# Attention and FP4 feed-forward kernel: the mask of the transposed scores moved from TensorE to VectorE

## The chip, the cores and the metric

The kernel runs on one core of one Trainium2 chip. The metric is the device time of one execution in microseconds (us). A core has five engines with queues of their own: TensorE (PE; its weight loads are listed as PEld), VectorE (DVE), ScalarE (ACT), GpSimd (POOL) and SyncE (SP), which here only issues DMAs. They wait for each other by semaphores alone.

## The reference

`x` has 8 batches of 1024 rows of 512. With `xn` the layer norm of `x`, the result is `x + attention(xn) + ffn(xn)`.

```
qkv = xn @ W_attn + b_attn                    # 16 heads of 32
att = einsum('bhqd,bhkd->bhqk', q, k) * 32 ** -0.5
att = softmax(where(causal, att, -inf))
y   = einsum('bhqk,bhkd->bhqd', att, v)       # then @ W_proj + b_proj
ffn = fp4(silu(fp4(xn, w_gate)) * fp4(xn, w_up), w_down)
```

`fp4` quantises both of its operands in blocks of 16. The feed-forward part comes after the attention in the kernel and the change does not touch it.

## The kernel before, in words

`attention` loops over 8 batches. A batch first projects q, k and v, and then works through 8 pairs of heads (`PAIRS`), one after the other; after the last pair come the output projection and the start of the next batch. The order of the work in each engine is written out by hand in the engine's block.

For each pair the softmax needs two forms of the scores. The first gives the row maxima: for each of 16 tiles (`TILE`: 2 heads, 8 blocks of 128 queries, in the order of blocks 4, 3, 5, 2, 6, 1, 7, 0) `scores` (L727) computes 128 queries against all keys up to the diagonal, adds the causal mask by a matmul of an identity in bfloat16 with `causal`, which holds -1e30 above the diagonal (L747), and VectorE reduces the tile to minus its maximum (`row_max`, L494, reduction at L498). Two places in PSUM alternate: even tiles use `ps_s` (up to 1024 columns), odd ones `ps_dense[:, 0]` (up to 512). When a pair's 16 maxima are there, TensorE transposes them (`maxima`, L750), VectorE splits them into a high and a low part (`split_max`, L501), and two DMAs on SyncE's queue put them as two more rows under q (L321).

The second form is transposed, keys by queries, and has the maxima in it, so that ScalarE can take the exponential at once. For each of 8 steps (`kt`, a block of 128 keys; in the engines' loops the unit `u`) `transposed_scores` (L754) makes the parts listed in `PARTS`: per head up to 512 queries each, 4 parts in steps 0 to 3 and 2 parts in steps 4 to 7, 24 in all. The part that holds the diagonal block gets the mask by a further bfloat16 matmul (L764). The parts go through a ring of 3 PSUM banks (`ps_st`), from which ScalarE writes the exponentials (L663): for steps 0 to 4 into a ring of 3 places in SBUF (`pt`), for steps 5 to 7 into places of their own (`rob`). The parts with the higher queries come first, the diagonal block comes last.

The exponentials have two readers: `times_v` (L767, matmul at L776) multiplies them by v, step by step, steps 5 to 7 during the next pair; and the denominators are their sums over the keys. GpSimd adds the exponentials of steps 0 to 4 up in `stage` (`sum_up`, L422, additions at L434, a copy of the first block at L431), then `denominators` (L780, matmul at L793) sums that and steps 5 to 7 over the partitions in unit 1 of the next pair. VectorE copies the result out of PSUM (`copy_den`, L509, L515), DMAs spread it, VectorE inverts it (`invert`, L519), DMAs spread the inverse, and `divide` (L526, L535) scales the product in unit 7.

In the loop over units each engine takes its share of several pairs: while pair p's transposed scores are made, `beside(p, u)` deals the maxima's tiles of the pairs ahead, two per unit (`SHARE`): the last 8 tiles of pair p + 1 in units 0 to 3, the first 8 of pair p + 2 in units 4 to 7 (`M_UNIT` is 3). In pair 7 VectorE also normalises four tiles of the next batch's x (`norm`, L473, L475), in pair 6 it takes their statistics (`stats`, L464).

## Time and profile before

| | us |
|---|---|
| median of 3 runs (4161.25 to 4167.64) | 4165.79 |
| the profiled execution | 4181.09 |
| its span, first to last instruction | 4179.3 |
| TensorE busy | 3883.4 |
| VectorE busy | 2601.6 |
| ScalarE busy | 1221.1 |
| GpSimd busy | 930.7 |

The span is the time between the first and the last instruction of the program; the execution's own time adds what lies around it. Busy times are sums over the whole span, attention and feed-forward together; matmuls overlap each other in the records, so that TensorE's busy time is no measure of how full it is. The granted clock of TensorE is given as a share of full speed: 1.00 is 2.4 GHz, 0.5 is 1.2 GHz. In a row of the timeline, "x3" stands for three like instructions that were merged, and the square brackets tell how long the engine sat idle before and which instruction released it.

### The profile page before, as it was taken

The page shows a single profiled execution, that of the slowest core. Times are in us where ns is not written, and L with a number is a line of the kernel's source. Part 1 is how long each engine was busy: PE and PEld are TensorE (multiplying, and loading weights), DVE is VectorE, ACT ScalarE, POOL GpSimd, SP SyncE. Part 2 cuts the span into 40 slices and gives each one's busy share as a digit, 9 for nine tenths or more (in the row PEclk, how much of TensorE's full clock was granted, in tenths as well). Part 3 has the DMA queues.
Part 4 walks back from the last instruction along what each step waited for, and adds up shares of the span by engine and source line. Part 5 has one row for each costly group of instructions (what it writes and reads, how often), then busy time and mean ns, then how long its engine had stood idle before and what let it go on. Part 6 is the DMA issues. An engine that isn't in the chain of part 4 may idle for free. (4 is left out here: it accounts for less than half of the span.)

```text
span 4179.3 us, 63450 instructions
## 1 busy us (share of the span) xinstructions
PE 3883.4 (93%) x21836; PEld 2759.2 (66%) x21836; DVE 2601.6 (62%) x3683; ACT 1221.1 (29%) x2295; POOL 930.7 (22%) x464
## 2 busy tenths in 40 slices
PE   7999999999999999999999934999999999999998
PEld 5556556556556565565565523888888888888887
DVE  4554654654654645645545477777777777777776
ACT  2341441432432423513414422222222222222221
POOL 0451550551542533613514500000000000000000
PEclk9999999999999999999998956999999999999999
DMA  4414324324325234234144121110011000100010
GB/s 152 105 47 152 91 62 152 87 73 142 74 90 138 71 105 128 56 129 119 41 152 93 44 76 43 31 32 30 30 35 33 30 30 30 37 31 30 30 35 28
DMA packets 161754, 302.38 MB, mean 72 GB/s; under 512 B 41072, under 2 KB 43120, under 8 KB 161520
## 3 DMA queue, kind: packets, MB, share of 16 engines
q1 hardware_dynamic: 143088, 265.79, 22.7%
q10 hardware_dynamic: 18432, 33.56, 2.5%
q8 instruction: 135, 2.21, 0.2%
q14 instruction: 99, 0.81, 0.1%
HBM read 196.61 MB, written 101.13 MB: 71 GB/s over the span
## 5 line engine op out<-in xcount | busy, mean ns | idle before, releaser
L1252 PE MATMUL f_ps<-wgu,xqt 128*128 128x512 f32 (+1 forms) x4608 | 992.5, 373 | 17.4 <-DVE h L1107 14.6
L1252 PEld LDWEIGHTS f_ps<-wgu,xqt 128*128 128x128 f32 x4608 | 841.1, 188 | 153.8 <-DVE h L1107 30.0
L498 DVE TENSOR_REDUCE mx<-ps_s 128x1 f32<-128x640 f32 (+3 forms) x576 | 552.5, 959 | 288.0 <-PE ps_s L747 281.1
L663 ACT ACTIVATE pt<-ps_st 128x512 f32<-128x512 f32 (+3 forms) x1152 | 549.3, 527 | 613.8 <-PE ps_st L764 381.2
L434 POOL TENSOR_TENSOR stage<-stage,pt 128x1536 f32<-128x1536 f32 (+2 forms) x176 | 518.0, 2943 | 16.5 <-ACT pt L663 1.1
L1262 PE MATMUL f_ps_o<-wd,hqt 128*128 128x512 f32 x2112 | 512.4, 395 | 2.2 <-DVE hqt L1114 2.2
L1262 PEld LDWEIGHTS f_ps_o<-wd,hqt 128*128 128x128 f32 x2112 | 392.6, 189 | 80.9 <-DVE hqt L1114 2.6
L722 PE MATMUL ps_dense<-arena,wa 128*128 128x512 f32 x1536 | 399.9, 406 | 9.5 <-DVE rob L546 8.0
L498 DVE TENSOR_REDUCE mx<-ps_dense 128x1 f32<-128x512 f32 x448 | 218.7, 488 | 247.7 <-PE ps_dense L747 247.7
L722 PEld LDWEIGHTS ps_dense<-arena,wa 128*128 128x128 f32 x1536 | 283.4, 191 | 74.3 <-issue 12.2
L761 PE MATMUL ps_st<-stack 98*128 98x512 f32 (+3 forms) x768 | 315.4, 440 | 5.1 <-ACT pt L663 5.1
L761 PE MATMUL ps_st<-arena 98*128 98x512 f32 (+3 forms) x768 | 299.1, 432 | 17.5 <-ACT pt L663 16.1
L434 POOL TENSOR_TENSOR stage<-pt 128x1792 f32<-128x1792 f32 x64 | 257.2, 4019 | 101.3 <-ACT pt L663 101.3
L638 ACT ACTIVATE stage<-ps_dense,bqk 128x512 fp32r<-128x512 f32 x128 | 88.1, 689 | 604.4 <-PE ps_dense L722 604.4
L431 POOL TENSOR_TENSOR stage<-pt,ones 128x256 f32<-128x256 f32 x64 | 39.3, 614 | 999.5 <-ACT pt L663 603.6
L764 PE MATMUL ps_st<-identb,causal 128*128 128x128 bf16 x1024 | 248.0, 243 | 0.0
L761 PEld LDWEIGHTS ps_st<-arena 98*128 98x128 f32 x768 | 149.1, 207 | 138.2 <-ACT pt L663 89.3
L745 PE MATMUL ps_s<-stack 96*128 96x512 f32 (+1 forms) x576 | 185.3, 396 | 56.9 <-DVE mx L498 30.7
L857 PE MATMUL ps_dense<-wp,yt 128*128 128x512 f32 x512 | 224.5, 594 | 2.1 <-DVE rob L546 2.0
L1182 ACT ACTIVATE silu<-f_ps 128x512 f32<-128x512 f32 (+1 forms) x192 | 107.0, 557 | 373.7 <-PE f_ps L1252 373.7
L761 PEld LDWEIGHTS ps_st<-stack 98*128 98x128 f32 x768 | 152.7, 213 | 95.3 <-ACT pt L663 53.0
L663 ACT ACTIVATE rob<-ps_st 128x384 f32<-128x384 f32 (+2 forms) x384 | 144.8, 384 | 207.1 <-PE ps_st L764 202.8
(121 smaller groups left out, 5044.1 us busy)
## 6 DMA issues: line engine op xcount, KB each, us to landing
qk_scratch<-stage SPq DMA_DIRECT2D x128, 512.0 KB, 3.0
stack<-qk_scratch SPq DMA_DIRECT2D x192, 256.0 KB
arena<-qk_scratch SPq DMA_DIRECT2D x192, 256.0 KB
xs<-in_L_attn_x SPq DMA_DIRECT2D x64, 256.0 KB, 3.1
rob<-in_L_attn_x ACTq DMA_DIRECT2D x64, 256.0 KB, 2.8
acc_scratch<-rob ACTq DMA_DIRECT2D x64, 256.0 KB, 2.2
xt<-in_L_attn_x SPq DMA_DIRECT2D x64, 256.0 KB, 2.6
at<-acc_scratch SPq DMA_DIRECT2D x64, 256.0 KB, 2.6
```

The lines of the kernel that those rows point to most:

```text
L434: nc.gpsimd.tensor_tensor(both[:, :, cols], (ring(0) if kt == 1 else both)[:, :, cols], ring(kt)[:, :, cols], ALU.add).then_inc(summed_up, 1)
L498: nc.vector.tensor_reduce(mx[:, h * ST + q:h * ST + q + 1], scores_bank(p, n)[:, 0:(q + 1) * P], axis=AX.X, op=ALU.max, negate=True).then_ ...
L638: nc.scalar.activation(stage[:, i % 2, 0].bitcast(F32R), bank("QK", i), ACT.Identity, bias=bqk[:, r * G + g:r * G + g + 1]).then_inc(qk_hi, 1)
L663: nc.scalar.activation(a[:, q - first * P:q - first * P + n], ps_st[:, w % ST_RING, 0:n], ACT.Exp, scale=SCALE).then_inc(st_exp, 1)
L722: last = nc.tensor.matmul(bank(*use), left(lh, k), right(rh, k), start=n == 0, stop=n == len(terms) - 1)
L745: last = nc.tensor.matmul(out[:, k0:k1], qs, stack(p)[0:KS, 2 + h, k0:k1], start=True, stop=k1 < keys)
L761: last = nc.tensor.matmul(out, stack(p)[0:KM, 2 + h, kt * P:(kt + 1) * P], stack(p)[0:KM, h, q:q + n], start=True, stop=not diagonal)
L764: last = nc.tensor.matmul(out[:, 0:P], causal[:, :], identb[:, :], start=False, stop=True)
L857: last = nc.tensor.matmul(bank("P", k), yt[:, g, t * P:(t + 1) * P], wp[:, g, :], start=g == 0, stop=g == G - 1)
L1182: nc.scalar.activation(silu[:, c, 0:n], ps[:, [0, 1, 1][c], 0, 0:n], ACT.Silu).then_inc(s_done, 1)
L1252: last = nc.tensor.matmul(ps[:, [0, 1, 1][c], gu, 0:n], xqt[:, a, k], wgu[:, b, gu, k, f:f + n], start=i == 0, stop=i == len(terms) - 1)
L1262: last = nc.tensor.matmul(ps_o[:, :], hqt[:, a, k], wd[:, b, k], start=i == 0, stop=i == len(terms) - 1)
```

## The change

- `transposed_scores` makes one matmul per part; the masks at L764 are gone. In their place VectorE takes, after the exponential, the minimum of the diagonal blocks of both heads (2 x 128 columns) and a constant `seen` in bfloat16, which is 0 where a key lies behind the query and the largest number elsewhere (`clean`). `times_v` and `sum_up` wait for it.
- The parts with the lower queries, and so the diagonal block, come first in `PARTS`.
- The exponentials of steps 0 to 3 have fixed places, step 4 takes step 1's. ScalarE waits for the readers of each place; GpSimd sums in the order 1, 0, 2, 3, 4.
- The maxima's masks are a function of their own (`mask_scores`) and follow the scores later: behind another part, or two tiles' masks one after the other.
- The tiles are dealt as 2, 3, 3, 2, 2, 2, 2, 0 per unit, `M_UNIT` is 2; the split of the maxima and the inversion come in unit 3, the normalisations of pair 7 in unit 2.
- ScalarE instead of VectorE copies the denominators.

```diff
@@ -41,12 +42,17 @@
     PARTS = [[(h, max(c * QC, kt * P), (c + 1) * QC - max(c * QC, kt * P))
-              for c in reversed(range(NQ)) if (c + 1) * QC > kt * P for h in range(2)] for kt in range(ST)]
+              for c in range(NQ) if (c + 1) * QC > kt * P for h in range(2)] for kt in range(ST)]
     NPARTS = sum(len(parts) for parts in PARTS)
     PART0 = [sum(len(parts) for parts in PARTS[:kt]) for kt in range(ST + 1)]
-    ST_RING, PT_RING, SLOTS, XR = 3, 3, 4, 4
+    ST_RING, SLOTS, XR = 3, 4, 4
     RINGED = 5
+    PT0 = {}
+    for kt in range(RINGED - 1):
+        PT0[kt] = 2 * P * sum(ST - k for k in range(kt))
+    PT0[RINGED - 1] = PT0[1]
+    PT_COLS = 2 * P * sum(ST - k for k in range(RINGED - 1))
     TAIL0 = {kt: 2 * P * sum(ST - k for k in range(RINGED, kt)) for kt in range(RINGED, ST)}
...
@@ -54,19 +60,22 @@
+    SUM_ORDER = [1, 0, 2, 3, 4]
+    FREED = {0: 2, 1: 1, 2: 3, 3: 4, 4: 5}
     SUMS = sum(summed(p) for p in range(PAIRS))
     TILE = [(h, q) for h in range(2) for t in range(ST // 2) for q in (ST // 2 + t, ST // 2 - 1 - t)]
-    SHARE = TILES // ST
-    M_UNIT = ST // 2 - 1
-    EARLY = TILES - SHARE * (M_UNIT + 1)
+    SHARE = [2, 3, 3, 2, 2, 2, 2, 0]
+    M_UNIT = 2
+    EARLY = TILES - sum(SHARE[:M_UNIT + 1])
     DEN_UNIT = 1
     def beside(p, u):
-        first = TILES + EARLY + p * TILES + SHARE * u
-        return [divmod(n, TILES) for n in range(first, first + SHARE) if n < PAIRS * TILES]
+        first = TILES + EARLY + p * TILES + sum(SHARE[:u])
+        return [divmod(n, TILES) for n in range(first, first + SHARE[u]) if n < PAIRS * TILES]
...
@@ -399,6 +408,8 @@
             pool.wait_ge(consts, 2)
+            pool.affine_select(out=seen[:, :], in_=seen[:, :], compare_op=ALU.is_ge, fill=0.0,
+                               base=0, pattern=[[1, P]], channel_multiplier=-1).then_inc(consts, 1)
             pool.wait_ge(b_load, 4 * DMA)
...
@@ -422,26 +433,27 @@
                     pool.wait_ge(st_exp, ONE + b * PAIRS * NPARTS + p * NPARTS + PART0[kt + 1])
+                    pool.wait_ge(cleaned, ONE + b * PAIRS * ST + p * ST + kt + 1)
                     if kt > 1:
                         pool.wait_ge(summed_up, ONE + b * SUMS + p * RINGED + kt)
+                    both = stage[:, :, :, :].rearrange("p h a n -> p h (a n)")
                     cols = slice(kt * P, S)
-                    both = stage[:, :, :, :].rearrange("p h a n -> p h (a n)")
-                    ring = lambda k: pt[:, (p * RINGED + k) % PT_RING]
                     if kt == 0:
-                        nc.gpsimd.tensor_tensor(both[:, :, 0:P], ring(0)[:, :, 0:P], ones[:, 0:1].unsqueeze(2).to_broadcast([P, 2, P]),
+                        nc.gpsimd.tensor_tensor(both[:, :, 0:P], exps(0)[:, :, 0:P], ones[:, 0:1].unsqueeze(2).to_broadcast([P, 2, P]),
                                                 ALU.mult).then_inc(summed_up, 1)
+                    elif kt == 1:
+                        nc.gpsimd.tensor_tensor(both[:, :, cols], exps(0)[:, :, cols], exps(1), ALU.add).then_inc(summed_up, 1)
                     else:
-                        nc.gpsimd.tensor_tensor(both[:, :, cols], (ring(0) if kt == 1 else both)[:, :, cols], ring(kt)[:, :, cols],
-                                                ALU.add).then_inc(summed_up, 1)
+                        nc.gpsimd.tensor_tensor(both[:, :, cols], both[:, :, cols], exps(kt), ALU.add).then_inc(summed_up, 1)
                         inv_std(b + 1, 0, XR)
-                    for kt in range(summed(p)):
-                        if kt == 0 and p:
-                            pool.wait_ge(den_full, ONE + b * PAIRS + p)
+                    if p:
+                        pool.wait_ge(den_full, ONE + b * PAIRS + p)
+                    for kt in SUM_ORDER[:summed(p)]:
                         sum_up(p, kt)
...
@@ -506,13 +518,11 @@
-                def copy_den(p):
-                    if p == 0:
-                        dve.wait_ge(o_out[0], ONE + b * (ST // 2) * DMA)
-                    else:
-                        dve.wait_ge(y_div, ONE + b * PAIRS * 2 + p * 2)
-                    dve.wait_ge(den_full, ONE + b * PAIRS + p + 1)
-                    nc.vector.tensor_copy(dn, den_bank(p)).then_inc(den_copy, 1)
+                def clean(p, kt):
+                    dve.wait_ge(st_exp, ONE + b * PAIRS * NPARTS + p * NPARTS + PART0[kt] + 2)
+                    nc.vector.tensor_tensor(exps(kt)[:, :, 0:P], exps(kt)[:, :, 0:P], seen[:, :].unsqueeze(1).to_broadcast([P, 2, P]),
+                                            ALU.min).then_inc(cleaned, 1)
...
@@ -581,17 +591,22 @@
                         tiles = beside(p, u)
+                        if u == M_UNIT + 1 and p + 1 < PAIRS:
+                            split_max(p + 1)
+                        late = len(PARTS[u]) == 2
+                        if late and len(PARTS[u - 1]) == 2:
+                            clean(p, u - 1)
                         for n in tiles[:1]:
                             row_max(*n)
-                        if u == DEN_UNIT and p:
-                            copy_den(p - 1)
+                        if not late:
+                            clean(p, u)
                         for n in tiles[1:]:
                             row_max(*n)
-                        if u == M_UNIT and p + 1 < PAIRS:
-                            split_max(p + 1)
-                        if u == M_UNIT and p:
+                        if u == ST - 1:
+                            clean(p, u)
+                        if u == M_UNIT + 1 and p:
                             invert(p - 1)
-                        if p == PAIRS - 2 and not final and u > M_UNIT:
+                        if p == PAIRS - 2 and not final and 0 <= u - M_UNIT - 1 < XR:
                             stats(b + 1, u - M_UNIT - 1)
...
@@ -645,11 +660,13 @@
                     for kt in range(ST):
-                        before = p * RINGED + kt - PT_RING
-                        if kt < RINGED and before >= 0:
-                            pp, pk = divmod(before, RINGED)
-                            act.wait_ge(pv_done, ONE + b * PAIRS * ST + pp * ST + pk + 1)
-                            act.wait_ge(summed_up, ONE + b * SUMS + pp * RINGED + max(pk, 1) + 1)
+                        if kt == RINGED - 1:
+                            act.wait_ge(pv_done, ONE + b * PAIRS * ST + p * ST + 2)
+                            act.wait_ge(summed_up, ONE + b * SUMS + p * RINGED + FREED[1])
+                        elif kt < RINGED and p:
+                            last = RINGED - 1 if kt == 1 else kt
+                            act.wait_ge(pv_done, ONE + b * PAIRS * ST + (p - 1) * ST + last + 1)
+                            act.wait_ge(summed_up, ONE + b * SUMS + (p - 1) * RINGED + FREED[last])
                         if kt == RINGED:
...
@@ -658,9 +675,15 @@
                             w = p * NPARTS + PART0[kt] + i
-                            a, first = exps(p, kt, h)
+                            if kt == DEN_UNIT and p and i == len(PARTS[kt]) - 1:
+                                if p == 1:
+                                    act.wait_ge(o_out[0], ONE + b * (ST // 2) * DMA)
+                                else:
+                                    act.wait_ge(y_div, ONE + b * PAIRS * 2 + (p - 1) * 2)
+                                act.wait_ge(den_full, ONE + b * PAIRS + p)
+                                nc.scalar.activation(dn, den_bank(p - 1), ACT.Copy).then_inc(den_copy, 1)
                             act.wait_ge(st_full, ONE + b * PAIRS * NPARTS + w + 1)
-                            nc.scalar.activation(a[:, q - first * P:q - first * P + n], ps_st[:, w % ST_RING, 0:n], ACT.Exp,
+                            nc.scalar.activation(exps(kt)[:, h, q - kt * P:q - kt * P + n], ps_st[:, w % ST_RING, 0:n], ACT.Exp,
                                                  scale=SCALE).then_inc(st_exp, 1)
...
@@ -742,10 +767,13 @@
                         k1 = min(k0 + 512, keys)
-                        last = nc.tensor.matmul(out[:, k0:k1], qs, stack(p)[0:KS, 2 + h, k0:k1], start=True,
+                        nc.tensor.matmul(out[:, k0:k1], qs, stack(p)[0:KS, 2 + h, k0:k1], start=True,
                                                 stop=k1 < keys)
-                    last = nc.tensor.matmul(out[:, q * P:keys], identb[:, :], causal[:, :], start=False, stop=True)
-                    last.then_inc(s_full, 1)
+                def mask_scores(p, n):
+                    h, q = TILE[n]
+                    nc.tensor.matmul(scores_bank(p, n)[:, q * P:(q + 1) * P], identb[:, :], causal[:, :], start=False,
+                                     stop=True).then_inc(s_full, 1)
...
@@ -756,31 +784,27 @@
                     pe.wait_ge(st_exp, ONE + b * PAIRS * NPARTS + max(w - ST_RING + 1, 0))
-                    out = ps_st[:, w % ST_RING, 0:n]
-                    diagonal = q == kt * P
-                    last = nc.tensor.matmul(out, stack(p)[0:KM, 2 + h, kt * P:(kt + 1) * P],
-                                            stack(p)[0:KM, h, q:q + n], start=True, stop=not diagonal)
-                    if diagonal:
-                        last = nc.tensor.matmul(out[:, 0:P], causal[:, :], identb[:, :], start=False, stop=True)
-                    last.then_inc(st_full, 1)
+                    nc.tensor.matmul(ps_st[:, w % ST_RING, 0:n], stack(p)[0:KM, 2 + h, kt * P:(kt + 1) * P],
+                                     stack(p)[0:KM, h, q:q + n], start=True, stop=True).then_inc(st_full, 1)
                     pe.wait_ge(st_exp, ONE + b * PAIRS * NPARTS + p * NPARTS + PART0[kt + 1])
+                    pe.wait_ge(cleaned, ONE + b * PAIRS * ST + p * ST + kt + 1)
                     for s in range(2):
                             last = nc.tensor.matmul(by_tile(y_bank(p)[y_rows(h, s), y_cols(kt, s)]), v_head(kt, p, h),
-                                                    exps_of_parity(p, kt, h, s), start=kt == 0, stop=kt == ST - 2 + s)
+                                                    exps_of_parity(kt, h, s), start=kt == 0, stop=kt == ST - 2 + s)
                     last.then_inc(pv_done, 1)
                     if p + 2 < PAIRS:
-                        pe.wait_ge(s_max, ONE + b * PAIRS * TILES + (p + 2) * TILES + EARLY + SHARE * DEN_UNIT)
+                        pe.wait_ge(s_max, ONE + b * PAIRS * TILES + (p + 2) * TILES + EARLY + sum(SHARE[:DEN_UNIT]))
                     for kt in range(summed(p) - 1, ST):
...
@@ -816,22 +840,29 @@
                     scores(1, n)
+                    mask_scores(1, n)
                 for p in range(PAIRS):
                         parts = len(PARTS[u])
-                        early = (parts + 1) // 2
-                        for i in range(early):
+                        ahead = 2 if u == M_UNIT else 1
+                        for i in range(parts // 2):
                             transposed_scores(p, u, i)
+                            if u == M_UNIT and i < ahead:
+                                for n in tiles[i:i + 1]:
+                                    scores(*n)
                         if u == M_UNIT + 1 and p + 1 < PAIRS:
                             maxima(p + 1)
-                        for n in tiles[:1]:
-                            scores(*n)
-                        for i in range(early, parts):
-                            if i < parts - 1 or parts == 2:
-                                transposed_scores(p, u, i)
+                        if u != M_UNIT:
+                            for n in tiles[:ahead]:
+                                scores(*n)
+                        if parts > 2:
+                            transposed_scores(p, u, 2)
+                        for n in tiles[:ahead]:
+                            mask_scores(*n)
                         if u == DEN_UNIT and p:
...
@@ -839,10 +870,11 @@
                             times_v(p, u - 1)
-                        if parts > 2:
-                            transposed_scores(p, u, parts - 1)
-                        for n in tiles[1:]:
+                        transposed_scores(p, u, parts - 1)
+                        for n in tiles[ahead:]:
                             scores(*n)
+                        for n in tiles[ahead:]:
+                            mask_scores(*n)
                 for kt in range(RINGED, ST):
```

## Rows read from the trace of the kernel before

**Rows 1.** The page: span, and busy time of the engines with share and instructions.
```profile
span 4179.3 us, 63450 instructions
...
PE 3883.4 (93%) x21836; PEld 2759.2 (66%) x21836; DVE 2601.6 (62%) x3683; ACT 1221.1 (29%) x2295; POOL 930.7 (22%) x464
```

**Rows 2.** Windows of one pair and of one batch: us, PE, PEld, DVE, ACT, POOL busy, PEclk.
```profile
178.20:202.00 23.80, 22.68 (x173) 13.01 (x169) 14.57 (x23) 10.91 (x24) 13.38 (x6) 0.93 0.36 81
1370.50:1392.70 22.20, 21.09 (x171) 12.21 (x169) 14.54 (x23) 10.91 (x24) 13.34 (x6) 1.00 0.40 88
...
432.60:734.90 302.30, 287.18 (x1753) 174.71 (x1753) 159.75 (x248) 102.18 (x216) 116.07 (x56) 0.93 0.36 99
734.90:1028.30 293.40, 278.66 (x1753) 170.70 (x1754) 159.79 (x248) 102.04 (x216) 116.06 (x56) 0.97 0.37 102
```

**Rows 3.** Groups by line: count | busy us, mean ns | idle before, releaser.
```profile
L764 PE MATMUL ps_st<-identb,causal 128*128 128x128 bf16 x1024 | 248.0, 243 | 0.0
```

**Rows 4.** Timeline of pair 2, TensorE: start us, us, engine, line, operation.
```profile
174.35 0.48 PE L745 MATMUL ps_dense<-arena 96*128 96x512 f32 x1
...
174.72 0.48 PE L761 MATMUL ps_st<-arena 98*128 98x512 f32 x1
...
179.43 0.71 PE L761 MATMUL ps_st<-arena 98*128 98x512 f32 x2
```

**Rows 5.** VectorE groups by shape: two reductions, an operation on SBUF alone.
```profile
L498 DVE TENSOR_REDUCE mx<-ps_s 128x1 f32<-128x1024 f32 x128 | 156.7, 1225 | 95.4 <-PE ps_s L747 95.4
...
L498 DVE TENSOR_REDUCE mx<-ps_dense 128x1 f32<-128x256 f32 x112 | 47.0, 419 | 45.0 <-PE ps_dense L747 45.0
...
L981 DVE TENSOR_TENSOR xq<-xd,xsc 128x512 f32<-128x512 f32 x64 | 44.3, 693 | 2.2
```

**Rows 6.** GpSimd groups by shape: the five sums of a pair.
```profile
L434 POOL TENSOR_TENSOR stage<-pt 128x1792 f32<-128x1792 f32 x64 | 257.2, 4019 | 101.3 <-ACT pt L663 101.3
L434 POOL TENSOR_TENSOR stage<-stage,pt 128x1536 f32<-128x1536 f32 x64 | 222.0, 3468 | 6.5 <-ACT pt L663 1.1
L434 POOL TENSOR_TENSOR stage<-stage,pt 128x1280 f32<-128x1280 f32 x56 | 163.5, 2920 | 5.1 <-POOL stage L434 0.5
L434 POOL TENSOR_TENSOR stage<-stage,pt 128x1024 f32<-128x1024 f32 x56 | 132.5, 2365 | 4.8
...
L431 POOL TENSOR_TENSOR stage<-pt,ones 128x256 f32<-128x256 f32 x64 | 39.3, 614 | 999.5 <-ACT pt L663 603.6 <-PE ps_dense L793 395.9
```

**Rows 7.** Timeline near 294.7 and 296.1; and line 475: ns min/median/max of 64.
```profile
292.00 4.00 POOL L434 TENSOR_TENSOR stage<-pt 128x1792 f32<-128x1792 f32 x1 [1.13 <-ACT pt L663]
...
294.69 1.60 DVE L475 TENSOR_SCALAR xs<-xs,mv 128x512 f32<-128x512 f32 x1
...
296.08 3.51 POOL L434 TENSOR_TENSOR stage<-stage,pt 128x1536 f32<-128x1536 f32 x1
...
296.21 3.66 DVE L475 TENSOR_SCALAR xs<-xs,mv 128x512 f32<-128x512 f32 x1
...
L475 DVE TENSOR_SCALAR xs<-xs,mv x64: 533/537/3681, 30.3 to 2137.8; 128x512 f32<-128x512 f32 x64
```

**Rows 8.** Timeline 268 to 301: VectorE with one operand in SBUF, under GpSimd's sums.
```profile
278.90 8.92 POOL L434 TENSOR_TENSOR stage<-stage,pt 128x1536 f32<-128x1536 f32 x3
...
281.33 0.28 DVE L506 TENSOR_TENSOR mr<-ps_dense,mr 16x128 fp32r<-16x128 f32 x1
```

**Rows 9.** Timeline of pair 2: GpSimd's first sum starts, the maxima's transpose.
```profile
179.93 4.03 POOL L434 TENSOR_TENSOR stage<-pt 128x1792 f32<-128x1792 f32 x1 [1.12 <-ACT pt L663]
...
185.69 0.33 PE L752 MATMUL ps_dense<-ident,mx 128*128 128x128 f32 x1
```

**Rows 10.** Timeline of pair 7: the product with v of step 3 starts.
```profile
298.78 1.07 PE L776 MATMUL ps_y<-pt,v 128*32 128x256 f32 x6
```

**Rows 11.** Timeline of pair 6: the inversion, and the division that waits for its result.
```profile
281.54 0.23 DVE L519 RECIPROCAL inv<-den 128x16 f32<-128x16 f32 x1
...
287.92 1.41 DVE L535 TENSOR_TENSOR yt<-ps_y,rob 64x512 f32<-64x512 f32 x2 [2.99 <-DMA rob<-inv_scratch]
```

## What I predict, and why

> **What bounds the kernel now.** I read the page first. The span is 4179.3 us and the profiled execution took 4181.09 us, 15.3 more than the median of the runs shown (4165.79); the sum below is made against 4181.1 and moved by that. TensorE is busy for 93% of the span, VectorE 62%, GpSimd 22% [rows 1]. The change touches only the attention part, and there the eight batches of eight pairs repeat, so I next took windows of one pair [rows 2]. In the middle of a batch (pairs 1 to 5) a pair takes 22.2 us at full clock and 23.8 us where TensorE's granted clock falls to half for a while (0.93 in the mean). Batches fall in two kinds as well, 293.4 us at 0.97 and 302.3 us at 0.93. Of a pair's 22.2 us TensorE shows 21.1 busy, VectorE 14.5, ScalarE 10.9, GpSimd 13.3. So TensorE bounds the pair, with about 1 us of waits in it, and VectorE has 7.7 us to spare, spread in small idle pieces.
>
> **The masks of the transposed scores (removed).** Two per step, 16 per pair, 1024 in all, 243 ns each in the table [rows 3]; as matmuls overlap, their price is the distance between starts. A scores matmul of 512 columns starts at 174.35 and the next matmul, behind a mask, at 174.72: 0.37 us apart. Two of 512 columns without a mask between them take 0.71 together where one takes 0.48, so 0.23 apart [rows 4]. A mask costs 0.14 us. 16 x 0.14 = 2.2 us per pair, 143 us over 64 pairs: what TensorE gives back if nothing else comes to bound it.
>
> **Maximum masks together.** They stay 16 per pair, and only in steps 1 and 2 do two stand side by side; the second then saves its 0.1 us of switching, 0.2 per pair. But the first mask of such a pair now waits behind the second tile's scores, so its reduction starts later. I book nothing.
>
> **The minimum (added to VectorE).** 8 per pair, 512 in all, on 2 x 128 columns. An operation of 512 columns on SBUF takes 0.69 us, just what a reduction of 512 would take between the two in the table, and a reduction of 256 takes 0.42 [rows 5]. So 0.42 each, 3.4 per pair; the copy of the denominators, 512 columns and so another 0.69, leaves. VectorE's load becomes 14.5 + 3.4 - 0.7 = 17.2 us per pair. ScalarE's becomes 10.9 + 0.7 = 11.6 of over 21 (at VectorE's price; at twice it 12.3), and the copy sits before an exponential whose scores TensorE issues only after the denominators and a product with v: nothing.
>
> **What the minimum waits for.** This decides. GpSimd's five sums take 4.02, 3.47, 2.92, 2.37 and 0.61 us, 13.4 per pair [rows 6], and the minima of steps 2 to 5 come due while they run. Around 294.7 VectorE normalises four tiles from SBUF to SBUF. Alone such an operation takes 0.53 us. The first is issued at 294.69 and takes 1.60, ending 0.3 after GpSimd's sum ended (292.00 + 4.00); the second takes 3.66, from 296.21 to 299.87, ending 0.3 after the next sum (296.08 + 3.51) [rows 7]. It is held for as long as GpSimd's instruction lasts. A subtraction with one operand in PSUM and one in SBUF, issued in the middle of GpSimd's 8.92 us of sums, takes 0.28 and waits for nothing [rows 8]. The minimum has both operands and its result in SBUF, and no row shows such an operation beside GpSimd. Its bounds are thus no wait (as in rows 8) and the whole rest of GpSimd's instruction (as in rows 7). I take the second, since an operation that touches SBUF alone is nearest to the normalisation. The Trainium skill (SBUF — State Buffer, Who interferes with whom) says that a VectorE instruction with two SBUF inputs contends with a GpSimd instruction that reads SBUF, and that the later one blocks fully. The trace has that for another operation (1.60 and 3.66 for 0.53); without the rule the sum would be that of the first rival below.
>
> **One pair laid out by hand.** Zero is the start of GpSimd's first sum. TensorE's instructions keep their distances, less the masks; reductions are interpolated between the two rows (0.29 for 128 columns to 1.23 for 1024). VectorE asks for the minimum of step 2 at 2.9, after three reductions; the sum holds it to 4.0; then two reductions of 1024 and 128 columns follow, and the transpose of the maxima, for which TensorE waits, is at 5.8. In the trace it is at 185.69 - 179.93 = 5.76 [rows 9], and there it stands one step further on in TensorE's order: the gain so far is eaten. Step 3's minimum is asked for at 7.7, while the sum of step 2 runs from 5.0 to 8.5. Step 4's at 11.1, the sum of step 3 running from 8.9 to 11.8. Step 5's at 13.8, the sum of step 4 running from 12.1 to 14.5. The waits are 1.1, 0.8, 0.7 and 0.6, in all 3.2 us. Each sum also waits for its step's minimum, so the two engines hold each other. Behind step 5's minimum VectorE has two reductions, two minima and the division (1.4), to 18.3, and one more reduction to 19.0, for which the scores of tile 10 wait. Masks, denominators, product with v, the last part and its exponential bring the next pair's zero to 23.7. Without the waits the same list closes at 21.2, not at 22.2 - 2.2 = 20.0: VectorE's 17.2 us lie in series with TensorE in places.
>
> **The sum.** Pairs 0 to 5: +1.5 each against 22.2, 48 pairs, +72 us. Pair 6 has half the reductions, but the chain sum, minimum, sum and product remains: I take +2 each, +16 (bounds -2, the masks' gain alone, and +3). Pair 7 carries the four normalisations, now in step 2 and thus in front of the minimum of step 3. By rows 7 one passes between two sums; the last ends some 9 us after the pair's first sum started, and the product of step 3 waits for it; before, it started at 298.78, 6.8 after 292.00 [rows 7, 10]. I take +2.5 in seven batches, +18 (bounds 0 and +5). Clock: half of the batches run at full clock now; with TensorE's load at 18.5 of 23.7 us I expect the half clock in all, which costs 23.8 - 22.2 = 1.6 in the 24 pairs that escape today, half of it hidden in waits: +20 (bounds 0 and +60). Exponentials in fixed places and GpSimd's order 1, 0, 2, 3, 4: step 3 no longer waits for a sum; the hand list has that already. The moved inversion, behind the reductions of step 3, runs at 10.8; its result came back 6.4 us later in the trace (281.54 to 287.92 [rows 11]), here at 17.2, and the division is due at 17: nothing. SyncE's queue keeps its order; the maxima's two DMAs start at 8 and have until the next pair's first scores at 14.5. In all +126: 4181 + 126 = 4307 for a profiled execution, 4291 for the median. I say 4290, own range 4210 to 4390.
>
> **Rivals.** *No hold.* If the minimum behaves as in rows 8, pairs 0 to 5 take 21.2 (-1.0 x 48 = -48), pair 6 gains 1.5 (-12), pair 7 loses as above (+18), the clock costs +20: about -20, 4145, with 4100 to 4185. For it: rows 8 is a two-operand operation. Against: one operand was in PSUM. *TensorE gets all of it back.* This is the faster side. Its place is the reductions of steps 2 and 3: if the minimum isn't held and VectorE is never more than half a microsecond behind TensorE there, the 143 us of masks return whole, and the third sum that step 3 waited for adds a little: 4166 - 143, about 4020. It decides from the point where the maxima's transpose comes under 4.5 us after the first sum. Against: 17.2 us of VectorE's work in a pair of 20. *Held, but hidden.* VectorE had 7.7 us idle; should the 3.2 us of waits fall into it rather than in front of a reduction that TensorE wants, the pair takes 22 and the time is 4130 to 4200. Against: the hand list has a reduction right behind every minimum.
>
> **Chances.** A measurement here tells 0.2% (8 us) from no change. Held and slower 0.62; no hold 0.13 (0.08 of it faster, 0.03 same, 0.02 slower); all back 0.12; held but hidden 0.13 (0.05 faster, 0.05 same, 0.03 slower). Together faster 0.25, same 0.08, slower 0.67. The range runs from 4110 to 4390: it leaves out the case of 4020, a little of "no hold", and the tail above.
>
> **What would show it.** Right: the minimum at 0.42 in steps 0 and 7 but 1 us and more in the mean, its ends just behind the ends of GpSimd's sums; a pair of 23 to 25 us; more half clock than before; mask groups of transposed scores gone. Wrong: the minimum's slowest under 0.6 us, which leaves the two rivals without a hold; or long minima with TensorE's waits on VectorE no longer than before.

## The result, and the profile after

The changed kernel takes 4402.14 us (median of 4 runs, 4395.46 to 4404.24); the kernel before takes 4163.52 beside it. The ratio is 1.0578, with a 95% interval of 1.0548 to 1.0607: 239 us slower. The forecast was 4290, with a range up to 4390: the sign and the mechanism came, the size is 112 us short. The profiled execution took 4401.85, which is 220.8 more than the profiled one of before.

Page of the kernel after: span, busy time of each engine, granted clock in 40 slices, and two of the costliest groups.

```profile
span 4400.0 us, 63096 instructions
...
PE 3904.3 (89%) x20812; PEld 2721.7 (62%) x20812; DVE 2916.3 (66%) x4139; ACT 1252.8 (28%) x2351; POOL 938.5 (21%) x466
...
PEclk9889989989889889989989985799999999999999
...
L447 POOL TENSOR_TENSOR stage<-stage,pt 128x1536 f32<-128x1536 f32 (+2 forms) x176 | 517.1, 2938 | 96.0 <-DVE pt L524 42.5
...
L445 POOL TENSOR_TENSOR stage<-pt 128x1792 f32<-128x1792 f32 x64 | 255.7, 3995 | 1185.8 <-ACT pt L686 1185.8
```

Against [rows 1], 1024 matmuls are gone and TensorE is busy for 89% instead of 93%, yet its busy time rose by 21 us: more of what is left runs at half clock (662 us of the span against 416, by the clock's records). GpSimd's own time grew by only 8 us: its sums are no slower (517.1 against 518.0 us in L447's three shapes), but they wait now (42.5 us) for the minimum. VectorE gained 315 us. Its groups by shape (busy us, mean ns of one, idle before):

```profile
L524 DVE TENSOR_TENSOR pt<-pt,seen 128x256 f32<-128x256 f32 x320 | 302.6, 946 | 93.3 <-ACT pt L686 91.8
L510 DVE TENSOR_REDUCE mx<-ps_s 128x1 f32<-128x1024 f32 x128 | 155.3, 1213 | 34.1 <-PE ps_s L775 34.1
...
L524 DVE TENSOR_TENSOR rob<-rob,seen 128x256 f32<-128x256 f32 x192 | 110.2, 596 | 33.8 <-ACT rob L686 31.5
```

The minimum (L524) was booked at 0.42 us plus waits. It takes 302.6 + 110.2 = 413 us, where 512 x 0.42 would be 215. The other 198 us aren't work, and the profile shows them as duration. The reduction of 1024 columns, which reads PSUM, stays at its price of before (1225 ns in [rows 5]).

One pair in the middle of a batch (pair 4 of batch 3) in the timeline. First GpSimd's five sums, then VectorE's minima of steps 2 to 5, then the transpose of the maxima (columns: start, duration; in brackets the idle time before and what ended it):

```profile
1215.42 4.00 POOL L445 TENSOR_TENSOR stage<-pt 128x1792 f32<-128x1792 f32 x1 [9.59 <-ACT pt L686]
1219.38 0.79 POOL L442 TENSOR_TENSOR stage<-pt,ones 128x256 f32<-128x256 f32 x1
1220.34 3.46 POOL L447 TENSOR_TENSOR stage<-stage,pt 128x1536 f32<-128x1536 f32 x1 [0.17 <-ACT pt L686]
1224.24 2.92 POOL L447 TENSOR_TENSOR stage<-stage,pt 128x1280 f32<-128x1280 f32 x1 [0.44 <-DVE pt L524]
1227.60 2.37 POOL L447 TENSOR_TENSOR stage<-stage,pt 128x1024 f32<-128x1024 f32 x1 [0.44 <-DVE pt L524]
...
1218.37 1.33 DVE L524 TENSOR_TENSOR pt<-pt,seen 128x256 f32<-128x256 f32 x1
...
1222.85 1.23 DVE L524 TENSOR_TENSOR pt<-pt,seen 128x256 f32<-128x256 f32 x1
...
1226.26 1.18 DVE L524 TENSOR_TENSOR pt<-pt,seen 128x256 f32<-128x256 f32 x1
...
1229.08 1.17 DVE L524 TENSOR_TENSOR rob<-rob,seen 128x256 f32<-128x256 f32 x1
...
1221.08 0.33 PE L780 MATMUL ps_dense<-ident,mx 128*128 128x128 f32 x1 [1.24 <-DVE mx L510]
```

Each minimum ends 0.28 us after the GpSimd instruction in front of it: 1219.70 after 1219.42, 1224.08 after 1223.80, 1227.44 after 1227.16, 1230.25 after 1229.97. And the sums of steps 3 and 4 wait for the minimum of their step (0.44 each). The excess over 0.42 is 0.91 + 0.81 + 0.76 + 0.75 = 3.23 us, where the hand list had 3.2. Over all pairs 0 to 5 it is 3.1 in the mean. The transpose starts 5.66 after the first sum (forecast 5.8), and TensorE idles 1.24 us before it, for a reduction.

Pair 6 of batch 0, the same step 3:

```profile
293.00 3.45 POOL L447 TENSOR_TENSOR stage<-stage,pt 128x1536 f32<-128x1536 f32 x1 [1.68 <-ACT pt L686]
...
293.62 3.11 DVE L524 TENSOR_TENSOR pt<-pt,seen 128x256 f32<-128x256 f32 x1
...
296.78 0.85 PE L800 MATMUL ps_dense<-pt,v 128*32 128x256 f32 x8 [2.01 <-DVE pt L524]
```

No maxima's reductions stand in front of the minimum here, so VectorE asks for it 0.6 us after the sum began rather than 2.5 us after. It is held 2.7 us, not 0.8, and TensorE stands for 2.01 of them. This batch is the clearer case: in the mean of eight, step 3's minimum is held 1.87 us in pair 6 and 1.03 in pairs 0 to 5, and all eight minima of a pair together 3.1 in both. Pair 7 of batch 0:

```profile
314.47 3.99 POOL L445 TENSOR_TENSOR stage<-pt 128x1792 f32<-128x1792 f32 x1 [9.21 <-ACT pt L686]
318.43 0.79 POOL L442 TENSOR_TENSOR stage<-pt,ones 128x256 f32<-128x256 f32 x1
319.30 3.49 POOL L447 TENSOR_TENSOR stage<-stage,pt 128x1536 f32<-128x1536 f32 x1
...
314.90 3.85 DVE L524 TENSOR_TENSOR pt<-pt,seen 128x256 f32<-128x256 f32 x1 [5.85 <-ACT pt L686]
318.67 0.83 DVE L487 TENSOR_SCALAR xs<-xs,mv 128x512 f32<-128x512 f32 x1
...
319.42 3.65 DVE L487 TENSOR_SCALAR xs<-xs,mv 128x512 f32<-128x512 f32 x1
...
323.91 0.41 DVE L524 TENSOR_TENSOR pt<-pt,seen 128x256 f32<-128x256 f32 x1
...
324.38 0.87 PE L800 MATMUL ps_y<-pt,v 128*32 128x256 f32 x4 [3.29 <-DVE pt L524]
```

Here step 2's minimum is held for GpSimd's first instruction, the first normalisation (0.83) for its second and the second (3.65) for its third; each ends 0.28 us after it. The product of step 3 starts 9.9 us after the first sum (forecast some 9; before 6.8 [rows 7, 10]), with TensorE idle for 3.29 us before it. So the chain had been seen, but its price was missed, as the windows of pairs 4, 6 and 7 of batch 3 show (after PE, PEld, DVE, ACT and POOL busy: granted clock, DMA share, GB/s; before, then after):

```profile
1114.20:1136.30 22.10, 20.99 (x170) 12.13 (x169) 14.54 (x23) 10.91 (x24) 13.38 (x5) 1.00 0.38 86
1158.50:1177.10 18.60, 17.95 (x150) 10.20 (x150) 12.47 (x28) 10.51 (x24) 10.61 (x4) 1.00 0.16 49
1177.10:1195.20 18.10, 16.49 (x131) 8.28 (x134) 9.42 (x10) 10.17 (x23) 12.11 (x7) 0.89 0.11 31
```

```profile
1206.50:1230.60 24.10, 20.04 (x154) 10.94 (x153) 19.15 (x30) 11.41 (x25) 13.50 (x5) 1.00 0.36 80
1254.90:1279.60 24.70, 19.77 (x134) 10.13 (x134) 17.30 (x36) 11.44 (x26) 13.46 (x5) 0.84 0.14 43
1279.60:1304.00 24.40, 17.89 (x115) 7.64 (x118) 13.45 (x16) 10.64 (x24) 9.52 (x5) 0.71 0.05 12
```

Pair 4 became 2.0 us longer, pair 6 became 6.1, pair 7 became 6.3. The waits of the product with v for the minimum, all new (us in total, times, longest):

```profile
PEld ps_y L800 <- DVE pt L524: 76.8, 47, 4.1
...
PE ps_y L800 <- DVE pt L524: 66.2, 51, 3.4
...
PEld ps_dense L800 <- DVE pt L524: 44.9, 35, 2.5
PE ps_dense L800 <- DVE pt L524: 41.9, 41, 2.0
```

The table gives all 64 pairs: the distance between the first exponentials of one pair and the next in the timeline (the last pair of a batch to its last exponential), mean of eight batches, pairs 0 to 5 averaged; then 8 x (6 x the first + the two others); and how much of that time, over all batches together, the granted clock was at half, by its records (pairs 0 to 5 / 6 / 7). "e" names are the experiments; each row is of the profiled execution alone.

| | pairs 0 to 5 | pair 6 | pair 7 | all | at half clock |
|---|---|---|---|---|---|
| before | 22.80 | 19.30 | 18.67 | 1398 | 128 / 10 / 45 |
| after | 24.87 | 25.28 | 25.77 | 1602 | 181 / 68 / 141 |
| e1 | 21.97 | 20.03 | 16.48 | 1347 | 65 / 0 / 0 |
| e2 | 21.34 | 19.75 | 16.08 | 1311 | 85 / 3 / 0 |
| e3 | 22.11 | 21.07 | 23.43 | 1417 | 102 / 12 / 90 |
| e4 | 24.75 | 24.60 | 22.95 | 1568 | 164 / 60 / 115 |
| e9 | 22.50 | 19.77 | 16.48 | 1370 | 158 / 0 / 0 |
| e13 | 21.71 | 18.93 | 16.50 | 1326 | 66 / 0 / 0 |
| e14 | 22.00 | 19.99 | 19.75 | 1374 | 68 / 0 / 50 |
| e15 | 22.18 | 19.76 | 19.67 | 1380 | 68 / 0 / 50 |
| e16 | 21.94 | 18.84 | 15.71 | 1330 | 89 / 0 / 0 |
| e17 | 21.69 | 19.15 | 17.24 | 1332 | 64 / 0 / 0 |

Two things help to read it. The kernel before was profiled in one of its longer executions (4181.09, where its medians are 4154 to 4166), so that the table shows more of a gap to it than the medians do. And that kernel also tells what the clock is worth: its 75 executions beside the experiments run from 4140 us at a mean granted clock of 0.960 to 4181 us at 0.949. Time at half clock is twice (1 - mean clock) of the time, and a straight line through the 75 gives 0.44 us of time for each us at half clock (correlation 0.98).

TensorE's idle time in a pair, summed up from the timeline in the same way, is 1.02, 0.61 and 1.45 us before (pairs 0 to 5, 6, 7) and 3.44, 5.09 and 6.28 after; 1.01, 2.46 and 5.01 of that end with a minimum.

### The profile page after: what moved, and what is told of

Same layout as the page of the kernel before. It is cut to its first block and busy times, and to the rows that moved or that the text cites. A ratio compares the mean times of both kernels' runs of the same rounds, so it can differ in the third digit from the quotient of the medians.

```text
span 4400.0 us, 63096 instructions
## 1 busy us (share of the span) xinstructions
PE 3904.3 (89%) x20812; PEld 2721.7 (62%) x20812; DVE 2916.3 (66%) x4139; ACT 1252.8 (28%) x2351; POOL 938.5 (21%) x466
## 5 line engine op out<-in xcount | busy, mean ns | idle before, releaser
L686 ACT ACTIVATE pt<-ps_st 128x512 f32<-128x512 f32 (+3 forms) x1152 | 569.9, 526 | 759.7 <-PE ps_st L787 755.1
L447 POOL TENSOR_TENSOR stage<-stage,pt 128x1536 f32<-128x1536 f32 (+2 forms) x176 | 517.1, 2938 | 96.0 <-DVE pt L524 42.5
L524 DVE TENSOR_TENSOR pt<-pt,seen 128x256 f32<-128x256 f32 x320 | 302.6, 946 | 93.3 <-ACT pt L686 91.8
L787 PE MATMUL ps_st<-arena 98*128 98x512 f32 (+3 forms) x768 | 308.8, 461 | 14.3 <-ACT pt L686 8.7
L787 PEld LDWEIGHTS ps_st<-arena 98*128 98x128 f32 x768 | 158.6, 225 | 176.7 <-issue 97.0
L800 PE MATMUL ps_y<-pt,v 128*32 128x384 f32 (+2 forms) x1280 | 180.2, 568 | 66.5 <-DVE pt L524 66.2
L800 PE MATMUL ps_dense<-pt,v 128*32 128x384 f32 (+2 forms) x1280 | 174.9, 567 | 41.9 <-DVE pt L524 41.9
```

What stands on the lines that cost most here:

```text
L447: nc.gpsimd.tensor_tensor(both[:, :, cols], both[:, :, cols], exps(kt), ALU.add).then_inc(summed_up, 1)
L524: nc.vector.tensor_tensor(exps(kt)[:, :, 0:P], exps(kt)[:, :, 0:P], seen[:, :].unsqueeze(1).to_broadcast([P, 2, P]), ALU.min).then_inc(cle ...
L686: nc.scalar.activation(exps(kt)[:, h, q - kt * P:q - kt * P + n], ps_st[:, w % ST_RING, 0:n], ACT.Exp, scale=SCALE).then_inc(st_exp, 1)
L787: nc.tensor.matmul(ps_st[:, w % ST_RING, 0:n], stack(p)[0:KM, 2 + h, kt * P:(kt + 1) * P], stack(p)[0:KM, h, q:q + n], start=True, stop=Tr ...
L800: last = nc.tensor.matmul(by_tile(y_bank(p)[y_rows(h, s), y_cols(kt, s)]), v_head(kt, p, h), exps_of_parity(kt, h, s), start=kt == 0, stop ...
```

## The experiments

The theory: VectorE's minimum is held as long as a GpSimd instruction runs, and behind it wait the reductions, TensorE's product with v and the next sum. Its rival: VectorE's added work in series, with whatever the other edits bring, is enough without a hold ("held" is an operation whose duration grows to the end of GpSimd's instruction). All edits are made to the changed kernel, except e6. The kernel before took 4157.7 us beside e1 to e4, 4155.3 beside e5, e6, e7 and e9, 4158.8 beside e8, e10, e11 and e12, 4154.4 beside e13 and e14 and 4165.8 beside e15 to e17; each ratio is against the one beside it, and runs of different sessions are compared by their ratios.

**e1. Everything but the moved mask.** The minimum goes, TensorE's masks come back.

```diff
-                    nc.tensor.matmul(ps_st[:, w % ST_RING, 0:n], ..., start=True, stop=True).then_inc(st_full, 1)
+                    last = nc.tensor.matmul(ps_st[:, w % ST_RING, 0:n], ..., start=True, stop=not diagonal)
+                    if diagonal:
+                        last = nc.tensor.matmul(ps_st[:, w % ST_RING, 0:P], causal[:, :], identb[:, :], start=False, stop=True)
+                    last.then_inc(st_full, 1)
```

> The changed kernel with the minimum taken out and TensorE's masks put back: only the new order of parts, the dealing of tiles, the fixed places, the later maximum masks and ScalarE's copy remain. Theory (GpSimd holds the minimum): the rest costs little, 4130 to 4210 us, pairs 6 and 7 back near 19 us each. Rival (the new order of the queues itself makes TensorE wait): most of the 238 us stays, over 4300 us.

Measured: 4125.04, ratio 0.9922 (0.9900 to 0.9943), 33 us faster than before. The rest of the change is a gain by itself, and all of the loss comes with the moved mask. The normalisations of pair 7 take 0.54 us each in this kernel (mean of 64), where they take 0.99 before and 0.91 in the change: none is held.

**e2. No minimum and no mask** (`clean` and the waits for it taken out).

> The changed kernel with neither minimum nor TensorE mask on the transposed scores (the causal mask is left out there). Theory: this is what TensorE can give back at most; 4166 - 143 = about 4020 us, with 3980 to 4080. Rival (TensorE is then bound by VectorE's reductions in the new order): 4100 us or more.

Measured: 4094.07, ratio 0.9828 (0.9755 to 0.9901). The 1024 masks are worth 31 us here, not 143. The kernel leaves the causal mask of the transposed scores out.

**e3. A reduction in place of the minimum**: the same 2 x 128 columns read, in the same place of VectorE's queue, with the same waits, but one input in SBUF only.

```diff
-                    nc.vector.tensor_tensor(exps(kt)[:, :, 0:P], exps(kt)[:, :, 0:P], seen[:, :].unsqueeze(1).to_broadcast([P, 2, P]),
-                                            ALU.min).then_inc(cleaned, 1)
+                    nc.vector.tensor_reduce(spare[:, kt], exps(kt)[:, :, 0:P], axis=AX.X, op=ALU.max).then_inc(cleaned, 1)
```

> In place of the minimum VectorE reduces the same 2 x 128 columns into a spare place: same queue place, same waits, about the same 0.42 us, but one operand from SBUF only. No mask is applied to the transposed scores, so the attention's result leaves the causal mask out there. Theory (hold): the operation is 0.42 us in all steps and the time falls to 4120 to 4200 us (hand list without waits: 21.2 us per pair). Rival (VectorE's added 3.4 us per pair in series, hold or not): 4350 us and more.

Measured: 4195.14, ratio 1.0093 (1.0080 to 1.0106). VectorE's groups of this kernel:

```profile
L525 DVE TENSOR_REDUCE spare<-pt 128x2 f32<-128x256 f32 x320 | 131.4, 411 | 86.2 <-ACT pt L686 84.7
...
L525 DVE TENSOR_REDUCE spare<-rob 128x2 f32<-128x256 f32 x192 | 74.4, 411 | 28.7 <-ACT rob L686 26.4
```

0.411 us in every step, beside GpSimd's sums or not. The same place in the queue, with no hold on the operation itself, costs 101 us more than no operation (e2) and 207 us less than the minimum. The 101 aren't all work in series: by the table 59 of the 106 between e2 and e3 lie in pair 7, where the normalisations in front of the reduction are held in this kernel (1.24 us in the mean, against 0.54 in e2). That is 45 us over the 64 of them.

**e4. The normalisations of pair 7 at the end of its steps** (`u == ST - 1` for `u == M_UNIT`), so that none stands in front of a minimum.

> The changed kernel with the four normalisations of pair 7 moved from step 2 to step 7, behind all minima. Theory: the product of step 3 no longer waits for them; pair 7 is 4 to 6 us shorter in seven batches, 30 to 40 us in all, 4360 to 4375 us. Rival (another wait takes over, the sum of step 2 holding the minimum of step 3): under 10 us.

Measured: 4379.33, ratio 1.0513 (1.0429 to 1.0597): 23 us less than the change (28 between the profiled executions). By the table pair 7 brings 23 (25.77 to 22.95, 8 times), the other pairs 11. There are two executions of e4, and the ratios' intervals of e4 and the change overlap. Less than expected: without the normalisations pair 7 is still 22.95, since the minimum itself is held there (step 2's for 3.85 us, step 3's for 0.83, in the mean of eight).

**e7. The minimum kept, GpSimd's sums cut to 128 columns per head.**

```diff
-                    cols = slice(kt * P, S)
+                    cols = slice(kt * P, (kt + 1) * P)
...
-                        nc.gpsimd.tensor_tensor(both[:, :, cols], both[:, :, cols], exps(kt), ALU.add).then_inc(summed_up, 1)
+                        nc.gpsimd.tensor_tensor(both[:, :, cols], both[:, :, cols], exps(kt)[:, :, 0:P], ALU.add).then_inc(summed_up, 1)
```

> The changed kernel, minimum and all, but each of GpSimd's sums takes 128 columns per head and not all that remain (0.6 us in place of 2.4 to 4.0); the rest of the sums is left out of the denominators. Theory (the minimum is held by GpSimd's instruction): the minima fall under 0.6 us in the mean and the time to that of the run with the reduction, 4170 to 4220 us. Rival (the long minima are VectorE's own, by operand types or addresses, or the loss lies in the order of the queues): minima stay near 0.9 us and the time over 4300 us.

Measured: 4148.08, ratio 0.9975 (0.9949 to 1.0000). VectorE's groups:

```profile
L524 DVE TENSOR_TENSOR pt<-pt,seen 128x256 f32<-128x256 f32 x320 | 135.3, 423 | 95.4 <-ACT pt L686 93.9
...
L524 DVE TENSOR_TENSOR rob<-rob,seen 128x256 f32<-128x256 f32 x192 | 75.8, 419 | 21.5 <-ACT rob L686 20.4
```

The same minimum, instruction for instruction, at 0.42 instead of 0.95 and 0.60. GpSimd's length is what held it, and some 250 us hang on that. The sums over the other columns are left out of the denominators. e3 and e7 take the hold away from opposite sides and agree in the main; e7 is the faster of the two by 1.2% of before. There the normalisations take 0.57 us in the mean and not 1.24, 43 us over the 64 of them, and the sums that others wait for are shorter as well.

**e6. The kernel before without its masks of the transposed scores.**

```diff
-                                            stack(p)[0:KM, h, q:q + n], start=True, stop=not diagonal)
-                    if diagonal:
-                        last = nc.tensor.matmul(out[:, 0:P], causal[:, :], identb[:, :], start=False, stop=True)
+                                            stack(p)[0:KM, h, q:q + n], start=True, stop=True)
```

> The kernel before with TensorE's masks of the transposed scores taken out and nothing in their place (the causal mask is left out there). Theory of the prediction: 0.14 us per mask come back whole, 143 us, 4015 us. Rival (as in the changed order, where masks were worth only 31 us: TensorE waits for exponentials and reductions instead): 4100 us or more.

Measured: 4128.26, ratio 0.9941 (0.9913 to 0.9969), so 27 us. The 143 us were never there to take, in the old order no more than in the new. Part of what is missing is the clock: the median of its executions is at a mean clock of 0.9505, the kernel before at 0.957 beside it, so that 52 us more are at half clock, some 23 us by the price above. In e2 it is 35 us more than in e1, some 15.

**e5. Half of each**: the minimum in steps 0, 1, 6 and 7, masks in steps 2 to 5, where the long sums run; the normalisations in step 7.

```diff
+        CLEANED = (0, 1, 6, 7)
...
+                    if kt not in CLEANED:
+                        return
```

> The changed kernel with the minimum in steps 0, 1, 6 and 7 only, where it was measured at 0.42 us, TensorE's masks in steps 2 to 5, and the normalisations in step 7. Theory (only held minima cost): as the run with all masks on TensorE or a little better, 4105 to 4150 us. Rival (VectorE's work in series costs whatever holds it): half of the 100 us between no mask and the reduction, 4150 to 4180 us.

Measured: 4134.59, ratio 0.9948 (0.9929 to 0.9966). Its minima:

```profile
L531 DVE TENSOR_TENSOR rob<-rob,seen 128x256 f32<-128x256 f32 x128 | 66.6, 553 | 77.2 <-ACT rob L693 77.2
...
L531 DVE TENSOR_TENSOR pt<-pt,seen 128x256 f32<-128x256 f32 x128 | 53.7, 420 | 6.6 <-ACT pt L693 5.1
```

Nearly no hold (17 us in all, in steps 6 and 7 of pair 6), and still it gains 0.5% where e1 gains 0.8%: 4 minima cost no less than the 8 masks beside them give back. The clock is lower, too: 0.961 in the median of the executions against 0.964, 26 us more at half clock, some 11 us by the price above, where e1 and e5 are 11 apart by their ratios. Why it is lower wasn't found.

**e9. e1 with each maximum mask right behind its scores.**

```diff
                                 scores(*n)
+                                mask_scores(*n)
```

> The rest of the change alone (TensorE's masks, no minimum), with each maximum's mask again right behind its scores. Theory (the later masks are worth the switching saved, 0.2 us per pair, less the later start of a reduction): within 10 us of the rest alone, 4115 to 4140 us. Rival (the later masks carry the gain of the rest): 4150 us or more.

Measured: 4123.91, ratio 0.9909 (0.9877 to 0.9941). In the median, setting the maximum masks together is worth nothing that can be told. But it may be two things that cancel: e1's five executions lie within 4123.53 to 4130.50, at clocks of 0.963 to 0.965, and e9's six run from 4111.34 at 0.964 to 4141.11 at 0.955. At the same clock e9 is the faster one, and it keeps that clock in one execution of six. In the profiled one (4141.11) pairs 0 to 5 have 158 us at half clock, where e1 has 65.

**e11. e1 with reductions of 128 columns only**, and **e10, the same without masks**: how much the masks are worth when VectorE has time.

```diff
-                    nc.vector.tensor_reduce(mx[:, ...], scores_bank(p, n)[:, 0:(q + 1) * P], axis=AX.X,
+                    nc.vector.tensor_reduce(mx[:, ...], scores_bank(p, n)[:, 0:P], axis=AX.X,
```

> The rest of the change alone (TensorE's masks), but every reduction of a maximum takes 128 columns only, 0.3 us in place of up to 1.2; the other columns are left out of the maxima. Theory (TensorE waits for reductions, so that taking masks away gives little): the time falls by 30 to 80 us to 4045 to 4095. Rival (TensorE's own work or the exponentials bound the pair): 4115 us or more.

> The same short reductions and no mask at all on the transposed scores. Theory (VectorE was the cover): now the masks are worth near their 143 us, at least 90 us less than the run with short reductions and masks. Rival (the exponentials and the ring of three banks cover them): the difference stays under 50 us, as it was 31 with whole reductions.

Measured: 4015.21 with masks (0.9652, 0.9593 to 0.9712) and 3955.77 without (0.9509, 0.9451 to 0.9568). The shorter reductions alone bring 110 us against e1: VectorE, busy for 61% of e1's span, does bound places of the pair. With them the masks are worth 59 us instead of 31, still not 143. So VectorE's reductions explain part of the lost value, and the clock a little (0.9725 without masks, 0.9755 with them, some 9 us); what takes the rest wasn't found.

**e12. e5 with the normalisations where the change puts them.**

> The minimum in steps 0, 1, 6 and 7, masks in steps 2 to 5, the normalisations in step 2 as in the changed kernel, where no minimum stands behind them until step 6. Theory: pair 7 falls from 18.7 to about 16.5 us in seven batches, 15 us off the run with the normalisations last: 4110 to 4128 us, level with the rest alone. Rival (the normalisations, held by GpSimd's sums, still reach the minimum of step 6): 4134 us or more.

Measured: 4138.50, ratio 0.9942 (0.9922 to 0.9961). A miss for the theory: I had put e5's small loss down to the place of the normalisations, and they aren't its cause: no normalisation is held in e12 (0.54 us in the mean), though the place is that of the change.

**e8. e1 with the denominators' copy on VectorE.**

> The rest of the change alone with the denominators' copy back on VectorE, where it stood before. Theory (the copy is hidden either way): within 10 us of the rest alone. Rival (VectorE in series): 0.7 us per pair in 48 pairs, 25 to 35 us more.

Measured: 4125.47, ratio 0.9917 (0.9890 to 0.9944). ScalarE or VectorE, the copy costs the same time: none.

**e13. e1 with the old deal.**

```diff
-    SHARE = [2, 3, 3, 2, 2, 2, 2, 0]
-    M_UNIT = 2
+    SHARE = [2] * ST
+    M_UNIT = ST // 2 - 1
```

> The rest of the change alone (masks on TensorE) with the tiles dealt as before: two per step, the maxima's transpose in step 4. Theory (the new deal gives the room): 15 to 35 us more than the rest alone, 4140 to 4160 us. Rival (the fixed places do): under 10 us.

Measured: 4108.20, ratio 0.9891 (0.9853 to 0.9929), where I had thought the new deal a gain. It takes 21 us from the pairs (1347 to 1326), 12 from pairs 0 to 5 and 9 from pair 6; the ratios' intervals of e13 and e1 overlap. With e16 below, which can't be told from it, this is the fastest version that computes the whole result.

**e14. e1 with ScalarE waiting in step 3 for the first two sums**, as the ring of three places made it wait.

```diff
+                        if kt == 3:
+                            act.wait_ge(summed_up, ONE + b * SUMS + p * RINGED + 2)
```

> The rest of the change alone, but ScalarE again waits with step 3's exponentials for GpSimd's first two sums, as the ring of three places made it. Theory (fixed places took a wait of 1.4 us per pair away, 89 us in the table of the kernel before): 15 us or more on top of the rest alone, 4140 us and more. Rival (it was hidden): under 10 us.

Measured: 4159.51, ratio 1.0009 (0.9989 to 1.0029). One wait gives back all of e1's gain, and by the total alone that would have been the cause. The table says otherwise: pairs 0 to 5 stay at 22.0 (before 22.8), and of the pairs pair 7 carries it alone, with 26 of the 43 us between the profiled executions. Another 12 lie between the batches, where the clock is at half for 28 us more. The waits of ScalarE for GpSimd, in the kernel before:

```profile
ACT pt L663 <- POOL stage L434: 88.9, 63, 1.9
```

and here:

```profile
ACT pt L684 <- POOL stage L441: 18.2, 8, 2.3
```

With the new deal step 3 comes so late that the wait exists in pair 7 only. So three more runs.

**e15. e13 with the same wait.**

> The change without the moved mask, with the old deal of the tiles, and ScalarE waits in step 3 for the first two of GpSimd's sums. In the run with the new deal the same wait brought the whole time back to that of the kernel before, but its pairs 0 to 5 stayed at 21.8 us (before 22.8) and pair 7 carried it alone (19.8 for 16.5), with 8 waits of 2.3 us. Theory (the wait for a place is what the rest of the change removes in pairs 0 to 5): with the old deal, where step 3 comes sooner, the wait shows in over 50 pairs and pairs 0 to 5 go to 22.5 and more, 4140 to 4160 us in all. Rival (something else in the rest of the change makes the pair shorter): pairs 0 to 5 stay at 21.6 to 21.9, the time is 4108 plus what pair 7 loses, 4108 to 4130.

Measured: 4159.32, ratio 1.0000 (0.9983 to 1.0017). The time is the theory's; the pairs 0 to 5, at 22.18, are neither at its 22.5 nor at the rival's 21.9 (e14's pairs, which the expectation puts at 21.8, are at 22.0 in the table).

```profile
ACT pt L684 <- POOL stage L441: 111.0, 56, 2.3
```

**e17. e15 with GpSimd's old order as well** (0 before 1, so that only one end is waited for, right behind the exponentials of step 1).

```diff
-    SUM_ORDER = [1, 0, 2, 3, 4]
-    FREED = {0: 2, 1: 1, 2: 3, 3: 4, 4: 5}
+    SUM_ORDER = [0, 1, 2, 3, 4]
+    FREED = {0: 2, 1: 2, 2: 3, 3: 4, 4: 5}
```

> As the old deal with the place's wait, and GpSimd sums in the old order, 0 before 1, so that the long sum that step 3 waits for ends 0.6 us later. Theory (the wait): at least as slow as with the order 1, 0, by up to 0.6 us in each of 48 pairs, 4145 to 4175 us, and the wait for a sum is over 60 us in total. Rival (something else): no slower than 4130 us.

Measured: 4119.69, ratio 0.9901 (0.9869 to 0.9933).

```profile
ACT pt L684 <- POOL stage L444: 90.0, 63, 1.7
```

This is the wait of before, as often and as long (88.9 us, 63 times), and pairs 0 to 5 stay at 21.69. It costs 0.1%, less than can be told: the wait came as the theory wanted it, and the loss didn't. With the new order of the sums (e15), where the wait also takes in the short sum, it costs 1.1%, half of it in pair 7 with 50 us at half clock.

**e16. e13 with the parts of the higher queries first.**

```diff
-              for c in range(NQ) if (c + 1) * QC > kt * P for h in range(2)] for kt in range(ST)]
+              for c in reversed(range(NQ)) if (c + 1) * QC > kt * P for h in range(2)] for kt in range(ST)]
```

> The change without the moved mask, with the old deal, and the parts with the higher queries first again. Theory (fixed places alone): the order of the parts is worth nothing, 4104 to 4112 us. Rival (the order of the parts carries some of the gain): 4120 us and more, pairs 0 to 5 above 21.9 us.

Measured: 4111.46, ratio 0.9883 (0.9851 to 0.9916): nothing in the time. Pairs 0 to 5 are at 21.94 in the profiled execution, just where the rival had them, with 23 us more at half clock than e13; pair 7 is shorter by 0.8.

## Why the prediction was right or wrong

The sum in measured terms, medians of one session except the change's: before 4158; the rest of the change -33 (e1); masks gone -31 (e2); an operation in the minimum's place +101 (e3), of which held normalisations are up to 45; the hold of the minimum +207 (the change). Together +244, beside the 239 of the direct comparison. Across these terms lies the clock: 246 us more at half clock between the profiled executions are worth some 108 of their 221 us by the price above, an estimate.

**The hold: right.** Four waits of 3.2 us in all per pair were forecast by [rows 7], and 3.1 are there in the mean. That [rows 8] would decide was the rival *no hold*, and the minima of the change (0.95 us in the mean of steps 0 to 4) and of e7 (0.42) refute it. By the rule of the Trainium skill (SBUF — State Buffer, Who interferes with whom) a VectorE instruction with two SBUF inputs that comes later than a GpSimd instruction that reads SBUF is blocked fully, and the trace agrees: 3.85 us for 0.42 in pair 7. A reduction with one SBUF input isn't held (0.411 us in e3), but a count of inputs isn't the whole of it: the normalisation has one tensor as its input, beside two columns of statistics, and is held (3.65 us for 0.53). Of the signs named beforehand one missed: all minima together take 0.81 us in the mean (413 us over 512), not 1 and more.

**Pairs 0 to 5: nearly right, but by luck: errors cancel.** The forecast was +72 and +20 for the clock (the hand list has TensorE's load as 18.5 us; 21.1 less 2.2 is 18.9); the table gives (24.87 - 22.80) x 48 = +99. Per pair: the rest of the change -0.8 (booked at nothing), masks -0.6 (booked at -2.2), added operation +0.8 (booked at +1.2), hold +2.8 (booked at +2.5). "A mask costs 0.14 us" holds as a distance between two starts, but "what TensorE gives back if nothing else comes to bound it" was then subtracted whole, and e6 shows that something else bound it even before the change. What the rest of the change gains isn't the wait for a sum, nor the order of the parts, the copy, the masks together or the deal (e17, e16, e8, e9, e13). What the record shows of it is the clock: 183 us of the pairs' time at half clock before, 65 in e1, and the difference at 0.44 is 52 us, where the pairs are 51 shorter. By the executions it is the same: medians of 0.9555 and 0.964 are 73 us at half clock apart, worth 32, and the medians of time differ by 33. Before, batches came in two kinds, 302.3 and 293.4 us [rows 2]; in e1 all are 290 to 292. In e9 two kinds are back, 287 to 291 and 300 to 301 us from the first exponential of a batch to that of the next, so the later maximum masks seem to have a part in it (one profiled execution each), though e9 has e1's median. Which other edit keeps the clock up wasn't found; the fixed places' other waits, for the product with v, and TensorE's new order around the tiles are what no run put back.

**The step that failed: pairs 6 and 7.** Booked were "+2 each, +16" for pair 6, with a bound of +3, and "+2.5 in seven batches, +18", with a bound of +5. Measured were +6.0 x 8 = +48 and +7.1 x 8 = +57: 71 us of the 95 by which the sum (+126) was short of the profiled executions' +221. Another 7 are in pairs 0 to 5. Some 16 more lie outside the pairs, 12 of them between the batches, where 81 us are at half clock and not 51. In pair 6 I reasoned that half of the reductions means half of the trouble. It doesn't: the minima of pair 6 are held for as long as those of the others (3.1 us), and the missing reductions had been the cover under which GpSimd's sum ran down before step 3's minimum was asked for (2.5 us into the sum in pair 4 of batch 3, 0.6 in pair 6 of batch 0). More of the hold is now in front of the product with v, and TensorE's idle time grows by 4.5 us in pair 6, by 2.4 in pairs 0 to 5. From e3 to the change pair 6 grows by 4.2 us, pairs 0 to 5 by 2.8. In pair 7 the delay of 3 us was seen rightly, but TensorE's idle time grows by 4.8, and I let the loss end with the wait. It doesn't: the clock falls behind it. The half clock grows by 58 and 96 us in these two pairs, at 0.44 some 68 us beside their 105. The windows of pairs 6 and 7 of a batch of e1:

```profile
1130.00:1150.00 20.00, 18.38 (x150) 10.08 (x149) 11.07 (x27) 11.32 (x26) 11.61 (x5) 1.00 0.17 52
1150.00:1166.50 16.50, 14.90 (x132) 7.35 (x135) 4.80 (x9) 10.63 (x25) 10.97 (x6) 1.00 0.07 18
```

Full clock in both, where the change has 0.84 and 0.71. And e3, where no minimum is held, has pair 7 at 23.43 with 90 us at half clock: an added operation behind the held normalisations is enough for that. So is the held minimum without the normalisations in front: from 16.08 in e2 pair 7 goes to 23.43 in e3, to 22.95 in e4, and with both to 25.77. The clock term of the prediction, +20, was worked out for the 24 pairs of full-clock batches and fits them (128 to 181 us); it had no part for pairs 6 and 7, though [rows 2] had shown that the clock falls in some batches and not in others. The windows of 4 us through pair 7 of batch 0 of the change, around the product at 324.38:

```profile
308.00:312.00 4.00, 4.00 (x31) 1.89 (x35) 0.42 (x1) 1.19 (x3) 0.00 (x0) 0.50 0.00 0
312.00:316.00 4.00, 3.55 (x25) 1.22 (x16) 1.10 (x1) 2.34 (x5) 1.53 (x1) 0.95 0.02 2
316.00:320.00 4.00, 2.16 (x13) 0.76 (x12) 4.00 (x3) 1.53 (x4) 3.92 (x3) 0.91 0.01 3
320.00:324.00 4.00, 1.08 (x2) 0.36 (x2) 4.00 (x4) 1.08 (x2) 2.79 (x1) 0.50 0.00 0
324.00:328.00 4.00, 2.80 (x14) 0.90 (x18) 0.91 (x3) 0.98 (x2) 0.00 (x0) 0.50 0.16 43
...
332.00:336.00 4.00, 4.00 (x40) 2.41 (x32) 0.96 (x2) 0.00 (x0) 0.00 (x0) 0.50 0.01 4
336.00:340.00 4.00, 4.00 (x34) 2.64 (x29) 2.54 (x1) 1.40 (x3) 0.00 (x0) 0.96 0.35 93
```

TensorE is busy for 2.16 and 1.08 us of 4 while VectorE stands full, held; the clock, which has just come back from half (it was there from 300 on at least, behind pair 6's wait of 2.01 us), goes to half (1.2 GHz) again and stays there until 336, also from 332 on, where TensorE is busy for all of the 4 us. That is the order of things in the trace; no run separated the cost of the wait from that of the clock.

**Copy and maximum masks: right in the total**, nothing each (e8, e9), the masks perhaps because a gain and a lower clock cancel (e9). **The other rivals.** *TensorE gets all of it back* (4020) fell with e2: with the hold and the work both gone it is 4094. *Held, but hidden* (4130 to 4200) fell by the waits of 1.24 to 3.29 us.

Open stay, beside the clock's cause: what keeps the masks cheap even beside short reductions (59 of 143 us came back), and why e5's clock is lower than e1's.

## What to carry to other kernels

Before work moves to VectorE, look at where its operands lie and what GpSimd does at that time: here an operation with two inputs in SBUF (0.42 us alone) lasted as long as the rest of GpSimd's instruction, up to 3.85 us, and what stands behind it in the queue is late too. A price per instruction, taken from the distance between two starts, was no more than an upper bound of what its removal brought (a fifth came back), and a pair with less work isn't one with less delay: ask what the missing work had covered, and what the clock does after a long wait. When an experiment reproduces a total, look whether it reproduces the places too (e14 didn't).

## What was not expected of the hardware

The hold is part of the instruction's own duration: VectorE's load looks 198 us heavier for work that didn't grow. One operation gets through between two GpSimd instructions: the normalisation that starts at 318.67 ends at 319.50, 0.28 us after the copy that began at 318.43, and the next is held for the whole sum (3.65). GpSimd pays little in return: its copy of 2 x 128 columns takes 0.80 us in the mean, 0.61 before. And single waits of 2 to 3 us per batch cost more than themselves: 2.3 us of ScalarE's waiting in pair 7 (e14) made that pair 3.3 us longer, with 6 us of each at half clock, and the kernel some 4 us longer per batch. The time of one and the same kernel follows the clock, too: 0.44 us for each us at half clock, over 75 executions that are up to 41 us apart.
